# First mixer of a two-layer network: sixteen key instructions go from VectorE to GpSimd, and four steps change their place

## The reference, cut to what matters

```python
xc = _causal_dwconv_silu(x, conv_w)          # 4 taps per channel, then SiLU
q, kg, v, g = xc @ wq, xc @ wkg, xc @ wv, xc @ wg + bg
gk = jax.nn.log_sigmoid(kg) / NORMALIZER      # decay of each key channel
k = 1.0 - jnp.exp(gk)
# per head: S = S * exp(gk_t) + k_t v_t ;  o_t = (q_t * scale) S
o = _gla(qh, kh, vh, gkh, scale)
o = o + jax.nn.sigmoid(aug_w[..., None] * vh)
o = (o - mu) * jax.lax.rsqrt(var + LN_EPS)    # per head
y = jax.nn.silu(g) * o @ wout
x = _layernorm(x + y)                         # and x @ w_g.T are the router's logits
```

## Time and profile before

| | |
|---|---|
| median of 3 runs | 4351.98 us (4350.99 to 4358.85) |
| profiled execution: its own time, its span | 4346.4 us, 4344.8 us |
| busy over the span: PE, DVE, ACT, POOL | 89%, 57%, 46%, 28% |
| mean granted TensorE clock | 0.947 of full |
| busy in one batch of the first mixer (47.78 us): PE, DVE, ACT, POOL | 40.34, 42.17, 29.57, 8.02 us |

### The profile page before, as it was taken

One profiled execution on the slowest core, in us unless ns is written; L12 is line 12 of the kernel. 1 busy time (PEld: TensorE's weight loads), 2 busy tenths in 40 slices (PEclk: granted clock), 3 DMA queues, 4 the chain that ended last, 5 costly groups with the idle time before them and its releaser, 6 DMA issues. The chain is left out here.

```text
span 4344.8 us, 69246 instructions
## 1 busy us (share of the span) xinstructions
PE 3884.9 (89%) x23860; PEld 2993.3 (69%) x23860; DVE 2465.0 (57%) x5456; ACT 1990.0 (46%) x4069; POOL 1196.7 (28%) x1878
## 2 busy tenths in 40 slices
PE   6788888598999999998489999999999999879998
PEld 3555555367888888887267777777777777656665
DVE  6888888462222222221568888888888887421111
ACT  5666666111211212211357777777777777432221
POOL 0111111101122122121345444455455453200000
PEclk8889989699999999999689999999999999889999
DMA  1011001154555555554211111111111111111111
GB/s 36 30 34 41 31 31 33 39 143 161 189 184 181 191 179 183 189 177 162 62 40 40 45 50 45 50 45 45 49 47 45 45 45 27 56 35 53 54 58 48
DMA packets 199445, 347.09 MB, mean 80 GB/s; under 512 B 75396, under 2 KB 150404, under 8 KB 180996
## 3 DMA queue, kind: packets, MB, share of 16 engines
q1 hardware_dynamic: 169284, 271.16, 19.6%
q0 software_dynamic: 29904, 72.65, 5.7%
HBM read 276.61 MB, written 68.16 MB: 79 GB/s over the span
## 5 line engine op out<-in xcount | busy, mean ns | idle before, releaser
L525 ACT ACTIVATE moe_rel<-moe_fc 128x512 f32<-128x512 f32 x284 | 169.5, 597 | 798.4 <-PE moe_fc L490 798.4
L490 PE MATMUL moe_fc<-moe_xT,moe_win 128*128 128x256 f32 x2272 | 503.7, 380 | 1.5 <-issue 0.8
L501 PE MATMUL moe_o<-moe_wout,moe_hT 128*128 128x256 f32 x2272 | 502.0, 379 | 0.0
L490 PEld LDWEIGHTS moe_fc<-moe_xT,moe_win 128*128 128x128 f32 x2272 | 432.7, 191 | 61.1 <-issue 2.1
L501 PEld LDWEIGHTS moe_o<-moe_wout,moe_hT 128*128 128x128 f32 x2272 | 426.4, 190 | 55.0
L549 DVE TENSOR_TENSOR moe_hT<-moe_rel 128x512 f32<-128x512 f32 x284 | 196.6, 692 | 360.7 <-ACT moe_rel L525 360.7
L1743 DVE SCALAR_TENSOR_TENSOR gdr_y<-gdr_bank,gdr_cw,gdr_y 128x511 f32<-128x511 f32 (+2 forms) x384 | 287.3, 748 | 37.3 <-ACT gdr_y L2056 22.9
L558 DVE COPY moe_osb<-moe_o 128x512 f32<-128x512 f32 x71 | 49.1, 691 | 425.0 <-PE moe_o L501 425.0
L2337 PE MATMUL gdr_bank<-gdr_hT,gdr_wqkv 128*128 128x512 f32 x512 | 258.2, 634 | 13.4 <-ACT gdr_qk L2071 7.8
L1305 PE MATMUL gdr_bank<-gdr_hT,gdr_wqkv 128*128 128x512 f32 x512 | 225.3, 599 | 3.5 <-ACT gdr_hT L1323 3.5
L1338 DVE TENSOR_TENSOR gdr_kb<-gdr_bank,gdr_x 128x512 f32<-128x512 f32 x32 | 20.6, 685 | 366.4 <-PE gdr_bank L1314 366.4
(11 more groups left out here) (393 smaller groups left out, 8786.2 us busy)
## 6 DMA issues: line engine op xcount, KB each, us to landing
moe_win<-in_moe_w SPq DMA_DIRECT2D x71, 1024.0 KB, 7.8
moe_wout<-in_moe_w SPq DMA_DIRECT2D x71, 1024.0 KB, 5.2
slots_out<-moe_osb POOLq DMA_DIRECT2D x71, 256.0 KB, 7.5
gdr_fz<-mixed_rows SPq DMA_DIRECT2D x18, 512.0 KB, 3.8
gla_xp<-in_xT_rows SPq DMA_DIRECT2D x16, 512.0 KB, 4.6
gla_xres<-in_x_rows SPq DMA_DIRECT2D x16, 512.0 KB, 3.7
token_rows<-gla_x POOLq DMA_DIRECT2D x16, 512.0 KB, 3.4
rt_W<-in_fc_b SPq DMA_DIRECT2D x32, 256.0 KB, 3.3
```

Source lines behind the costliest of these rows:

```text
L490: ins = nc.tensor.matmul(fc_ps[j][:, m % 2, :], win[u][:, c, m * P:(m + 1) * P], xT[:, c, :], start=(c == 0), stop=(c == DT - 1))
L501: ins = nc.tensor.matmul(o_ps[u][:, t, :], hT[u][:, k, t * P:(t + 1) * P], wout[u][:, k, :], start=(k == 0), stop=(k == FT - 1))
L525: nc.scalar.activation(rel[:, j, :, :], fc_ps[j][:], ACT.Relu).then_inc(relu_done, 1)
```

## The change

The eight differences and eight products of the keys are issued by GpSimd. GpSimd's loop becomes a written-out body with four parts: the power of the head norm, the store semaphore of the logits, the differences and products of the next batch, and the power, the row store and the logits' store of the past one. On DVE the centring and the variance of batch b stand at the end of body b and no longer at the start of body b + 1; the gate product opens the body; the first half convolution stays ahead of the second masked scores, with the variance no longer between; the residual sums come ahead of the last masked scores; row statistics and row scaling come around the third output. On ACT the squares move to the end of the body, and the head masking of the queries (`spread`) is split in two around a copy of values.

```diff
+                def head_rstd(b):
+                    wait, _ = waiter(pool, b)
+                    wait("var", 1)
+                    nc.gpsimd.tensor_tensor(rstd32[:], var32[:], mhalf[:], ALU.pow).then_inc(s["rstd"], 1)
+
+                def differences(b, u):
+                    wait, _ = waiter(pool, b)
+                    wait("G", 1)
+                    if later(b, 1):
+                        pool.wait_ge(s["sc"], (b - 1) * TT)
+                    for a in range(NSUB):
+                        n, r = SUB * (a + 1), SUB * a + SUB // 2 - 1
+                        nc.gpsimd.tensor_tensor(kt[u][:, :, a, 0:n], G[:, :, r:r + 1].broadcast_to([P, NCH, n]), G[:, :, 0:n],
+                                                ALU.subtract).then_inc(s["Dk"], 1)
+
+                def products(b, u):
+                    wait, _ = waiter(pool, b)
+                    wait("k", 1)
+                    for a in range(NSUB):
+                        n = SUB * (a + 1)
+                        wait("E", 5 + a)
+                        nc.gpsimd.tensor_tensor(kt[u][:, :, a, 0:n], kt[u][:, :, a, 0:n], k_[:, :, 0:n], ALU.mult).then_inc(s["kt"], 1)
...
+                def body(b, u, past, more, far):
+                    w = 1 - u
+                    if past is not None:
+                        head_rstd(past)
+                        if later(past, 0):
+                            logits_kept(past - 1)
+                    if more:
+                        differences(b + 1, w)
+                        products(b + 1, w)
+                    if past is not None:
+                        rows_out(past)
...
                 def body(b, u, past, more, far):
                     w, recur = 1 - u, inside(b)
                     if past is not None:
-                        head_norm(0, past, w)
+                        head_norm(2, past, w)
                     if far is not None:
                         conv(0, b + 2, u, far)
                     if recur:
                         masked(1, b, u)
-                    if past is not None:
-                        head_norm(1, past, w)
+                        outputs(0, b, u)
                     if more:
                         gates(b + 1)
-                    if recur:
-                        outputs(0, b, u)
...
                     if past is not None:
                         tail(0, past)
+                    if recur:
+                        masked(3, b, u)
                     if more:
-                        products(1, b + 1, w)
+                        products(b + 1, w)
                     if past is not None:
                         tail(1, past)
                     if recur:
-                        masked(3, b, u)
                         outputs(2, b, u)
-                    if more:
-                        products(2, b + 1, w)
+                    if past is not None:
+                        tail(2, past)
                     if far is not None:
                         conv(1, b + 2, u, far)
                     if recur:
                         outputs(3, b, u)
+                        head_norm(0, b, u)
                     if more:
                         own(b + 1, w)
+                    if recur:
+                        head_norm(1, b, u)
+                    if more:
                         masked(0, b + 1, w)
```

More of the change, by code:

```diff
@@ L737, in _, with logits_kept @@
                     pool.nop().then_inc(x1_free, 1)
+                def logits_kept(b):
                     pool.wait_ge(lg_stored, b * 16 + 16)
                     pool.nop().then_inc(lg_free, 1)
+                def body(b, u, past, more, far):
[9 more added lines that the diff above has]
+                        rows_out(past)
+                starts(body)
+                for b in range(2, B - 2):
+                    body(b, b % 2, b - 1, True, b // 2 + 1)
+                ends(body)
+                logits_kept(B - 1)
             @block.vector
@@ L774, in gates, with differences @@
                     done("gg", 1, ts(g[:], g[:], 1.0 / 16.0, GK_FLOOR, ALU.mult, ALU.max))
-                    Chain(dve, gate_step, b)(v.tensor_tensor_scan(flat(G[:]), flat(notstart[:]), g[:], 0.0, ALU.mult, ALU.add))
-                def differences(part, b, u):
+                    if later(b, 0):
+                        dve.wait_ge(s["Dk"], b * NSUB)
+                    done("G", 1, v.tensor_tensor_scan(flat(G[:]), flat(notstart[:]), g[:], 0.0, ALU.mult, ALU.add))
+                def differences(b):
@@ L789, in products @@
-                def products(part, b, u):
-                    wait, done = waiter(dve, b)
[L791 to L805, removed]
+                    ref8 = blocks8(G[:])[:, :, SUB // 2 - 1:SUB // 2].broadcast_to([P, NCH * NSUB, SUB])
@@ L958, in exponents @@
                         wait("gg", 1)
+                        if later(b, 0):
+                            act.wait_ge(s["kt"], b * NSUB)
                         done("ek", 1, a_op(ab[:], g[:], ACT.Exp))
                         done("k", 1, a_op(flat(k_[:]), ab[:], ACT.Copy, scale=-1.0, bias=1.0))
+                        wait("G", 1)
+                        done("E", 1, a_op(flat(eG[:]), flat(G[:]), ACT.Exp))
+                    elif part == 1:
                         wait("D", 1)
[L962 to L963 removed]
+                        done("E", 2, a_op(flat(eR[:]), flat(eR[:]), ACT.Exp))
                         wait("D", 2)
@@ L967, in exponents, with spread @@
                     else:
-                        for a in range(4 * (part - 1), 4 * part):
+                        for a in range(NSUB):
                             n = SUB * (a + 1)
-                            wait("D", 3 + a)
+                            wait("Dk", a + 1)
                             done("E", 5 + a, a_op(kt[u][:, :, a, 0:n], kt[u][:, :, a, 0:n], ACT.Exp))
-                def spread(b, u):
+                def spread(half, b, u):
                     wait, done = waiter(act, b)
                     wait("qt", 1)
-                    for h in range(GH):
+                    for h in range(half * GH // 2, (half + 1) * GH // 2):
                         ins = a_op(qspread[u][:, :, h, :], qt[:].rearrange("p (n i) -> p n i", i=SUB), ACT.Copy, scale=headmask[:, h:h + 1])
-                    done("spread", 1, ins)
+                    done("spread", half + 1, ins)
                 def values(t, b, u):
@@ L1031, in body @@
                         silu(b + 2, u)
+                    if inside(b):
+                        squares(b, u)
                     if more:
@@ L1078, in scores @@
                     if t == 0:
-                        wait("spread", 1)
+                        wait("spread", 2)
                         wait("kt", NSUB)
```

59 lines of the change are left out of this document (24 added, 35 removed).

## The result

The changed kernel takes 4277.16 us (median; 4271.99 to 4283.98), a ratio of 0.9821 to the kernel before, 95% interval 0.9806 to 0.9835. The forecast was 4292, range 4245 to 4350. One run of a later experiment, the doubled differences, took 5673.4 us against 4332 to 4352 for its other nine, and is left out of its median. In the profiled executions the whole went from 4346.4 to 4273.4 us and the first mixer's last logits copy on DVE from 843.2 to 764.2: the mixer gained 79, the stages behind it, which the change leaves alone, differ by 6 the other way.

A forecast was written before the change was run, and what follows sets the result against it. DVE bounds the first mixer, PE close behind: 36.85 + 5.4 + 0.6 + 0.9 = 43.75 us a batch against 47.78; 13 batches gain 52, ends 8, so 4346.4 - 60 = 4286, median 5.6 above: 4292, range 4245 to 4350.

The forecast's parts named there:

- 36.85 us of its own: First mixer: DVE's need a batch without its waits (3.20) and the key instructions (7.73), from 47.78 us.
- the keys' 7.73: First mixer: eight differences and eight products for the keys leave DVE, 7.73 us a batch.
- The collision: First mixer: ten DVE instructions with two SBUF operands wait for GpSimd's key instructions, 5.4 us a batch (5.0 to 5.8).
- No collision that counts: Rival, first mixer: moved work wholly hidden, PE becomes the bound, about 41.3 us a batch, time 4260; chance 0.20.
- The 84%: Later stage's trace: a DVE multiply was let in after 84% of a GpSimd product; used to price DVE's waits.
- DVE stands still: Rival, first mixer: DVE stands for all of GpSimd's key work, 51.3 us a batch, time 4390; chance 0.12.
- The 6.4: First mixer: DVE's loss a batch instead of 5.4 us if the port lock holds for the whole GpSimd instruction.
- GpSimd's price: First mixer: sixteen key instructions on GpSimd, 2.1 to 2.5 ns an element, 13.6 us a batch (12.6 to 14.6).
- the row power: First mixer: new DVE wait before scaling the rows, for GpSimd's power of 1.01 us; 0.6 us a batch.
- the last output: First mixer: DVE's wait for PE before the last output stays in part, 0.9 of 1.22 us.
- some 8 gained: First and last batches of the mixer: batch 0 loses some 5 us, start-up and run-out gain; some 8 us gained together.
- the waits' 3.2 less 1.5: First mixer: DVE's three waits (1.22, 0.52, 1.46) go, except 0.9 for an output and a new 0.6 for scaling.

The follow-up runs named there:

- order-only run: New order of VectorE and ScalarE, but the keys' differences and products on VectorE, against the kernel before: 4290.99 us, 0.9843, batch 44.54.

## Why the prediction was right, and where its sizes were off

- The bound and the base. DVE as the bound with 36.85 us of its own is shown by the order-only run, whose batch is that plus the keys' 7.73. (The 36.85 leaves out a fourth wait of before, 0.19 for the logits copy; it comes out right because the idle times of the four waits hold the ordinary gap of some 0.03 each.)
- The collision was put at 5.4 and is 4.96 in the batch shown; it disappears when GpSimd's instructions are cut to one element (for the pair of state updates also when they only write), and it stands in DVE's lengths, not in gaps. *No collision that counts* falls with that; its price holds: 4248 with the collision taken away, against 4260. The mechanism is as forecast, a wait for the rest of the GpSimd instruction under way, but the nearness of the size is in part luck: ten meetings of 0.54 us were forecast, and eight of 0.62 took place. The 84% was no share either: in the earlier trace rows the DVE multiply was let in 0.13 us ahead of the recorded end, much as the key instructions let DVE in, whatever their size.
- *DVE stands still* falls: 4.96 us for 14.2 of key work. The Trainium skill (SBUF — State Buffer, Who interferes with whom) states a lock for the whole instruction. The key instructions agree with it but for their last 0.14 to 0.21 us; the power of 5.51 us, beside which the pair keeps 1.01, does not. The 6.4 weighed for it counted the ten meetings, so 4.96 does not decide against the lock.
- GpSimd's price. The products cost 2.1 ns an element where DVE stood, the lower of the two prices forecast, the differences 1.7. The 14.2 us of key work hold GpSimd's own waits for DVE, such as the first difference's 1.33 for 0.29; 13.6 was forecast without them.
- Small waits: the row power 0.6 expected, 0.89 found; the last output 0.9 expected, 0.09 found; the second residual sum's 0.75 was not foreseen. 36.85 + 4.96 + 0.89 + 0.75 = 43.45 against 43.28 measured and 43.75 forecast.
- The mis-sized term is "some 8 gained" at the ends; where 60 us were forecast for the whole, the mixer gained 79. In place of it: the steady batches gave 12 x 4.20 = 50.4 of the mixer's 79, the last interval 7.7, the start (to the third sig product, 146.5 to 134.1) 12.4 and the run-out (75.6 to 67.0) 8.6. Order alone has 10.9, 8.0 and 6.0 of these three, so the order makes most of them. I had charged batch 0 with 5 us for GpSimd's keys in series: the first sig product comes at 59.7 before, 52.6 with order alone and 54.7 after, so GpSimd costs 2.1 there, and batch 0 gains 5.0 where a loss of 5 was forecast.
- What the prediction did not say: it set 7.73 saved against 5.4 paid and credited the moves with the waits' 3.2 less 1.5, but of the long power it said that it stood "at the head of the next body" and cost nothing; that cover hangs on the variance's move (with the norm back in its old place 1.48 of it shows). And it took the delay of ACT's exponentials as nothing, without naming the edit that makes it so, which the section on the change leaves out too: ScalarE's two copies of the turned outputs now go ahead of the exponentials, worth 4.8 us. GpSimd's keys are worth 1.0 us a batch in the new order (44.54 to 43.58), 1.4 in the old one with the copies first (47.78 to 46.40), and cost 3.4 without. (The copies first with the keys on VectorE was not run; before, PE has no wait listed for these copies.)

Open: why the power holds nothing, and how far a read of one operand, not of two, by GpSimd lengthens DVE.

## What to carry to other kernels

Work moved to a second engine is not saved by its time on the first: subtract what the two lose beside each other (here the rest of one GpSimd instruction for each DVE instruction that met one), and look in each in-order queue that consumes its result for what stands behind the consumer. Run the order without the move and the move without the order; here the order gave four fifths, and the move alone was a loss. When a slow engine's result is wanted soon, put instructions that do not need it between, which also takes them out of its reach.

## What the runs showed of the hardware

A GpSimd instruction that only writes (0.47 us for 512 elements a partition, 3.79 for eight) did not lengthen the VectorE pair beside it, while differences with two operands doubled it, 1.01 to 2.01. A VectorE instruction that met a difference or product under way began its own length 0.14 to 0.15 us (state updates 0.20 to 0.21) ahead of that instruction's recorded end, in all the kernels with these instructions in full size on GpSimd. Not only two operands count: in the run with each difference twice, the last step of the row statistics (L91, 128x4, one operand) took 0.51 us beside a product, against 0.17 in the kernel before. A power of 5.51 us held nothing.

GpSimd's differences undisturbed took 0.29 us at 64 elements and 0.95 at 448 (in the run with each difference twice), 1.7 ns an element; the products there, while VectorE stood, took 1.13 us at 448 and 1.26 at 512, which is 2.1 ns an element between 320 (0.85 us) and 512.
